# Ahead of a chunked recurrence: gate tables loaded during the projections, a growing recurrence, pipelined key products, first loads by need, key squares on ScalarE

## What is computed

```python
q, k, v = silu(hs @ Wq + bq), silu(hs @ Wk + bk), silu(hs @ Wv + bv)      # per token, 16 heads x 64
beta, fd, sd, fg, sg = five sigmoid gates per token and head
q = q * rsqrt(sum(q * q) + 1e-6);  k = k * rsqrt(sum(k * k) + 1e-6)
def step(S_f, S_s):                                                        # for each token
    S_f, S_s = fd * S_f, sd * S_s
    S_f = S_f + beta * k (v - k S_f);  S_s = S_s + beta * k (v - k S_s)
    S_fc, S_sc = cap(S_f + rf * S_s), cap(S_s + rf * S_f)
    o = fg * (q S_fc) + sg * (q S_sc)
```

## Time and profile before

| | us |
|---|---|
| runs, median of 3 | 3804.21 |
| profiled execution | 3796.57 |
| its span | 3794.8 |
| projections, first to last SiLU | 359.7 to 665.8 |
| gate stage, barrier to barrier | 688 to 970 |
| chunk loop, first PE instruction to last output | 1000 to 2777 |
| the rest of both layers behind it | 2777 to 3795 |

### The profile page before, as it was taken

The page is one execution under the profiler, slowest core; times in us unless marked ns, Lnnn a source line. Parts: engine busy times, 40 slices in busy tenths (PEclk is TensorE's granted clock), DMA queues, the critical chain, the costliest instruction groups (busy, mean ns, idle before and its releaser), DMA issues. The chain is left out here.

```text
span 3794.8 us, 75132 instructions
## 1 busy us (share of the span) xinstructions
PE 3016.8 (79%) x27767; PEld 2120.4 (56%) x27767; DVE 2638.0 (70%) x4556; ACT 1536.5 (40%) x3399; POOL 1485.2 (39%) x2134
## 2 busy tenths in 40 slices
PE   0666998572299998999989999999947368999898
PEld 0444433462277777777777777777737264333334
DVE  8895777399257775687847777566668737777775
ACT  0233888352033333333323333333325244555554
POOL 0000777473245554455545555455545513000000
PEclk9776999776589998899979998799979689999999
DMA  1001555654412321322232132122246342101111
GB/s 28 0 1 40 219 221 221 164 123 132 134 31 60 75 58 36 77 58 68 44 76 56 37 77 61 45 58 61 59 136 232 106 120 47 26 18 25 19 18 31
DMA packets 434170, 293.76 MB, mean 77 GB/s; under 512 B 335099, under 2 KB 396091, under 8 KB 425021
## 3 DMA queue, kind: packets, MB, share of 16 engines
q1 hardware_dynamic: 418976, 263.98, 24.9%
q0 software_dynamic: 10240, 8.41, 1.5%
q10 hardware_dynamic: 4608, 16.78, 1.4%
HBM read 159.59 MB, written 129.45 MB: 76 GB/s over the span
## 5 line engine op out<-in xcount | busy, mean ns | idle before, releaser
L2346 DVE TENSOR_REDUCE mx<-banks 128x2 f32<-128x1024 f32 (+3 forms) x384 | 360.4, 955 | 149.7 <-PE banks L1817 111.3
L2052 ACT ACTIVATE probs<-banks 128x1024 f32<-128x1024 f32 (+3 forms) x384 | 309.9, 810 | 287.0 <-PE banks L1839 156.6
L1083 ACT COPY xs<-banks 64x64 f32<-64x64 f32 (+2 forms) x640 | 166.2, 260 | 610.1 <-PE banks L924 607.1
L1573 POOL TENSOR_TENSOR prj_sq<-prj 128x1024 f32<-128x1024 f32 x64 | 218.2, 3428 | 389.8 <-ACT prj L1958 389.8
L924 PE MATMUL banks<-xc,ssm 64*64 64x16 f32 (+2 forms) x5120 | 262.3, 222 | 53.4 <-issue 43.1
L957 PE MATMUL banks<-stk,tw 128*128 128x192 f32 x1024 | 270.4, 423 | 38.8 <-DVE tw L1286 38.8
L802 POOL TENSOR_SCALAR xc<-xc,halves 128x64 f32<-128x64 f32 (+1 forms) x256 | 137.0, 535 | 411.0 <-DVE xc L1288 381.1
L924 PEld LDWEIGHTS banks<-xc,ssm 64*64 64x64 f32 x5120 | 220.6, 140 | 130.3 <-issue 67.7
L1288 DVE SCALAR_TENSOR_TENSOR xc<-xc,halves,banks 64x64 f32<-64x64 f32 (+1 forms) x512 | 160.4, 313 | 189.6 <-PE banks L935 185.6
L1700 PE MATMUL banks<-wproj,xnT 128*128 128x512 f32 x512 | 266.5, 602 | 20.3 <-ACT prj L1958 19.3
L1111 ACT COPY ah<-banks 128x768 f32<-128x768 f32 x128 | 102.2, 799 | 386.5 <-PE banks L957 386.5
(11 more groups left out here) (355 smaller groups left out, 7184.8 us busy)
## 6 DMA issues: line engine op xcount, KB each, us to landing
proj_s<-prj SPq DMA_DIRECT2D x32, 2048.0 KB, 6.3
qkv_t<-proj_s SPq DMA_DIRECT2D x32, 1536.0 KB, 6.7
ka<-proj_s ACTq DMA_DIRECT2D x32, 512.0 KB, 4.1
mem_s<-o_sb SPq DMA_DIRECT2D x32, 512.0 KB, 2.6
om<-mem_s SPq DMA_DIRECT2D x32, 512.0 KB, 3.9
om<-proj_s SPq DMA_DIRECT2D x32, 512.0 KB, 4.9
blk_s<-res SPq DMA_DIRECT2D x16, 512.0 KB, 4.6
rt_src<-r_s SPq DMA_DIRECT2D x512, 8.0 KB, 4.7
```

Of the source, the lines that this page charges most:

```text
L1573: pool.tensor_tensor(prj_sq[:, w, :], x, x, ALU.mult).then_inc(p_sq, 1)
L2052: act.activation(probs[:, s % 2, :, at:at + w], slot_of((kind, s, k))[:, :, 0:w], ACT.Exp, scale=D1 ** -0.5).then_inc(b_read, 1)
L2346: dve.tensor_reduce(mx[:, s % 2, c, :, t:t + 1].rearrange("p e a -> p (e a)"), slot_of((kind, s, k))[:, :, 0:w], AX, ALU.max).then_inc(a_r ...
```

## The change

- Gate loads move into the projections: after each of the first 16 tile stores SP issues four of them, `rf_c` comes with the weights, and the save of `res` comes ahead of the stores. The partition order becomes (odd or even head, pair, block). `gu` gets memory of its own.
- The key squares move from POOL to ACT, behind the fifth SiLU of a tile. `vv` is scaled in two parts (tiles 0 to 27 early), and PE's turns wait part by part.
- The gate recurrence runs over `w = 2 + t` columns in step t instead of all 18; POOL clears `gl` at the end of the projections. `lx` and its 4 MB store are gone: the two left rows are stored as they are (`l_s`), and the left factors of a tile are loaded into a cleared `lt_` by 16 small DMAs. `pc` and `yp` become seven prefix products `pq`, a masked sum and a correction. `invert(1)` leaves the stage; all parts from 1 on are inverted in the loop, in groups 0 to 10 of the 16 before their use.
- Key products: `kta` has two buffers, PE turns tile i + 1 before it multiplies tile i, ACT copies only the four 32 x 32 diagonal pieces (eight copies of 32 x 256), and POOL stores a tile with one DMA. A part is then loaded by 32 DMAs in place of one.
- The loads of tiles 0 and 1, and of `bd`, move into the gate stage, each after what it needs, and POOL's memsets move there with them. A tile's load is cut differently: 1 + 2 + 16 + 1 + 8 + 2 = 30 DMAs.
- Constants (`bmask`, `halves`, `rf_abs`, `one_rf`) are made ahead of the projections.

```diff
 # projections, SP
+            sp.dma_start(res_s, res[:, :, :].rearrange("p t d -> p (t d)")).then_inc(res_out, 16)
+            sp.wait_ge(g_stored, 16)
             for i in range(T):
                 ...
                 sp.dma_start(ps_v[i], prj[:, i % 4, :]).then_inc(p_stored[i % 4], 16)
+                for n in range(4 * i, min(4 * i + 4, 4 * H0)):
+                    k, h = n // H0, n % H0
+                    row = NB * (H0 // 2 * (h % 2) + h // 2)
+                    sp.dma_start(gu[row:row + NB, k, :, :], gates_s[(k + 1) * H0 + h, :].rearrange("(t j o) -> j t o", j=NB, o=SUB)).then_inc(gu_in, 16)
 # projections, POOL: one square instead of two, then
+            pool.wait_ge(p_silu, 8 * T)
+            pool.memset(gl[:, :, :, :], 0.0).then_inc(cc_set, 1)
 # projections, ACT
+                        if n == 4:
+                            act.wait_ge(p_silu, 8 * i + 4)
+                            act.activation(prj_sq[:, 1, :], prj[:, i % 4, HD:2 * HD], ACT.Square).then_inc(p_sq_q, 1)
 # gate stage, DVE, step t
-                seq.link(dve.tensor_tensor(ca[:, 0], src[:, 0], fd_, ALU.mult))
+                seq.link(dve.tensor_tensor(ca[:, 0, :, 0:w], src[:, 0, :, 0:w], fd_, ALU.mult))
 ...
-                seq.link(dve.tensor_tensor(gl[:, :, :, t], ca[:, 0], ca[:, 1], ALU.add))
+                seq.link(dve.tensor_tensor(gl[:, :, 0:w + 1, t], ca[:, 0, :, 0:w + 1], ca[:, 1, :, 0:w + 1], ALU.add))
 ...
-            invert(1)
 # a part's blocks, SP
-                sp.dma_start(nb, nblk_s[PT * c:PT * c + PT, :, :].rearrange("t u n -> u t n")).then_inc(nb_in, 16)
+                for j in range(NB):
+                    q, part_ = j // 2, slice(SUB * (j % 2), SUB * (j % 2) + SUB)
+                    for t in range(PT):
+                        sp.dma_start(nb[j:P:NB, t, :].rearrange("h (s o) -> h s o", o=SUB), nblk_s[PT * c + t, q, part_, :, part_].rearrange("s h o -> h s o")).then_inc(nb_in, 16)
 # gate stage, PE
+            turn_keys(0)
+            for i in range(T):
+                if i + 1 < T:
+                    turn_keys(i + 1)
+                key_products(i)
 # gate stage, ACT, copies of one tile
+                    for q in range(4):
+                        rows = slice(32 * q, 32 * q + 32)
+                        act.copy(ssa[rows, n, 8 * y:8 * y + 8, :].rearrange("p (h e) t -> p e h t", e=2),
+                                 banks[rows, 1024 + 1024 * y:2048 + 1024 * y].rearrange("p (e h t) -> p e h t", e=2, t=P)[:, :, :, rows]).then_inc(ss_kept, 1)
 # gate stage, POOL
+            for i in range(T):
+                n = i % 2
+                pool.wait_ge(ss_kept, 8 * i + 8)
+                pool.dma_start(nblk_s[i].rearrange("q r h o -> (q r) (h o)"), ssa[:, n, :, :].rearrange("p h o -> p (h o)")).then_inc(nblk_out[n], 16)
+                if i == ZERO_AT:                       # 22
+                    pool.wait_ge(gate_out, 32)
+                    pool.memset(cft[:, :, :], 0.0).then_inc(zero_set, 1)
+                if i in (ZERO_AT + 2, ZERO_AT + 4):
+                    y = (i - ZERO_AT) // 2 - 1
+                    pool.memset(blk[:, y, :, :, :], 0.0).then_inc(zero_set, 1)
 # gate stage, SP, in this order: load bd (24), load_tokens of tiles 0 and 1, load_part(0), pb and pball,
 # store gl and l_s, store_part(0), load_left x2, load_part(1), wait zero_set 3, load_blocks x2,
 # wait gate_set 1, store r_s of tiles 0 and 1, load_right x2, store the rest of r_s, wait gate_set 2,
 # 8 + 2 coefficient stores, wait for them, load_ends x2, pcb (2)
 # loop, SP, ahead of load_tile(i)
-                if i % PT == PT - 2 and 2 * PT - 2 <= i < T - PT:
-                    c = (i + 2) // PT
+                if i % PT == 0:
+                    c = i // PT
                     store_part(c)
                     if c + 1 < T // PT:
                         load_part(c + 1)
-                if i % PT == 0:
-                    sp.wait_ge(inv_out, 32 * (i // PT + 1))
+                    sp.wait_ge(inv_out, 32 * (c + 1))
                 load_tile(i)
 # loop, DVE: rows of the inverse of part k // 16 + 1 behind group k, q = k % 16
+        INVERSE = ((1, 2, 3), (4, 5, 6), (7, 8), (9,), (10,), (11,), (12,), (13,), (14,), (15,))
```

More of the change, by code:

```diff
@@ L668, in chunk_sync @@
+            sp.wait_ge(lm_set, MASKS)
+            for i in range(2):
+                load_left(i)
+            sp.wait_ge(inv_out, 32)
             load_part(1)
+            sp.wait_ge(zero_set, 3)
+            for i in range(2):
+                load_blocks(i)
             sp.wait_ge(gate_set, 1)
-            sp.dma_start(r_s.rearrange("h j r t s -> (h j) (r t s)"), rb[:, :, :, :].rearrange("p r t s -> p (r t s)")).then_inc(gate_out, 16)
-            sp.dma_start(l_s.rearrange("h (i r) t n -> (h i) (r t n)", r=2), lx[:, :, :, :, :].rearrange("p r t j o -> p (r t j o)")).then_inc(gate_out, 16)
@@ L672, in chunk_sync @@
[L672 to L679, removed]
@@ L680, in chunk_sync @@
-            end_phase(sp)
+            for first_, end in ((0, 2), (2, T)):
+                sp.dma_start(r_s[:, :, :, first_:end, :].rearrange("h j r t s -> (h j) r (t s)"), rb[:, :, first_:end, :].rearrange("p r t s -> p r (t s)")).then_inc(gate_out, 16)
+                if first_ == 0:
+                    sp.wait_ge(gate_out, 48)
+                    for i in range(2):
+                        load_right(i)
+            sp.wait_ge(gate_set, 2)
+            for e in range(2):
+                for k, src in enumerate((gam[:, 0], gam[:, 1], cend[:, 0], cend[:, 1])):
+                    sp.dma_start(cf_s[e, k].rearrange("g j t o -> (g j) (t o)"), src[64 * e:64 * e + 64].rearrange("p t o -> p (t o)")).then_inc(gate_out, 16)
@@ L1053, in chunk_act @@
+            for i in range(2):
+                load_keys(i)
+            keep_turned_keys(0)
+            for i in range(T):
+                if i + 1 < T:
+                    keep_turned_keys(i + 1)
+                keep_key_blocks(i)
             end_phase(act)
@@ L1189, in chunk_dve @@
             for m in range(2):
[L1190 to L1191 removed]
+                seq.link(dve.tensor_copy(pb[:, :, 2 * m:2 * m + 2], last[:, m, :, 0:2]))
+            dve.tensor_copy(glc[:, :, :, :], gl[:, :, 0:2, :]).then_inc(pb_set, 1)
             dve.wait_ge(pb_set, 1)
@@ L1245, in chunk_dve @@
             dve.wait_ge(lm_set, MASKS)
-            for lv in range(LEVELS):
-                q = P // (2 * SUB << lv)
-                seq.link(dve.tensor_reduce(half4[:, :, 0:q], ident[:, :].rearrange("p (q a t) -> p a q t", q=q, a=2), AX, ALU.add))
-                seq.link(dve.tensor_reduce(halves[:, lv, :], half4[:, :, 0:q], AX, ALU.add))
-            dve.scalar_tensor_tensor(out=rf_abs[:, :], in0=rf_c[:, :], scalar=-1.0, in1=rf_c[:, :], op0=ALU.mult, op1=ALU.max).then_inc(rf_set, 1)
+            dve.wait_ge(zero_set, 4)
@@ L1318, in new_state @@
                     dve.wait_ge(z_mm, k + 1)
+                if k == 4 and step == 0:
+                    dve.wait_ge(pc_in, 32)
                 if first(k):
```

364 lines of the change are left out of this document (183 added, 181 removed).

## The result

| | us | ratio to before [95% interval] |
|---|---|---|
| before, median beside it | 3803.88 | |
| after, median of 4 runs (3705.07 to 3714.81) | 3712.27 | 0.9754 [0.9737, 0.9771] |
| predicted | 3653, 3605 to 3700 | |

What follows compares the result with a forecast made beforehand. Bounds: a circle through GpSimd's key square in the projections, DVE's chain in the gate stage, PE in the loop. 174 us gained before the loop less 23 lost in it, 151 off 3796.6, plus 7.6 for the median: 3653, range 3605 to 3700.

Steps and rivals of the forecast that it cites:

- Key squares on ACT: Projections: ACT becomes the bound at 8.95 us a tile, 19.5 us saved, plus 2.5 in the last tile; no table loads.
- Tail: End of the projections: 7 us instead of 11.9 from DVE's last product to the barrier, 4.9 saved.
- Gate chain: Gate stage on DVE: recurrence 68.4 us against 101.5 before, chain ending 151 us after the stage starts.
- Key products and SP: Gate stage: key products 4.9 us a tile, ending at S + 165; SP's queue bounds the stage at S + 179.
- rival A: Gate stage: key products keep their old pace, 6.1 us a tile, zero_set 3 comes 32 us later: 3685; chance 0.2.
- Late by 0 to 10 each, I take 3: +18: Loop, tiles 4, 8, ..., 24: part loads delay the tile's reload 3 us each, 18 us lost, from 0 to 60.
- slack of 7.5: Loop reloads: 7.5 us between the landing of a tile's loads and PE's turn, the other five 6 to 11.
- The inverse of part 1 in the loop: Loop: 21.7 us of new DVE work, mostly hidden, costing 5 us, from 0 to 12.
- B: Loop: the reload queue is 13 us late instead of 3 at six tiles, +60: 3713; chance 0.13.
- C: Loop, first-tile groups: PE's clock stays up, nine groups gain 4.5 us each, 40 in all: 3613; chance 0.14.
- D: Projections don't shorten, ACT still waiting for GpSimd through the value squares, +22: 3675; chance 0.06.
- E: Loop: the tile's load lasts 36 us instead of 22, 6.5 late at 30 tiles, slower than before: 3830; chance 0.03.

Runs made afterwards that it cites:

- e3: The changed kernel with the key squares back on GpSimd: 3730.72 us, ratio 0.9811.
- e8: e5 and e6 together, with GpSimd's clearing of lt, ssm and sqr spread over tiles 1 to 4 of the key products: 3574.10 us, ratio 0.9296.
- e5: e1 with part 1 loaded behind the gate stage's last barrier, inverse rows one group later, clearing of cft and blk earlier: 3641.26 us, ratio 0.9488.
- e1: The changed kernel with a tile's own loads issued ahead of the next part's 32 loads: 3617.40 us, on another chip 3650.43, ratio 0.9502 both times.
- e7: The changed kernel with 24 of a part's 32 loads ahead of the tile's loads and 8 behind: 3676.22 us, ratio 0.9674.
- e6: e1 with first-tile groups also issuing the 12 products of other groups, into columns nothing reads: 3584.25 us, ratio 0.9332.

## Why the prediction was wrong

- *Key squares on ACT: right.* 8.95 us a tile forecast, 8.85 measured, no idle in front of the root; e3 gives 25 us at the stage's start for 22 forecast. The Square brought no table load.
- *Tail: right in sum.* Barrier at 659.4, forecast 661.6. It opens 8.8 us behind DVE's last product (650.59), where I took 7; the tiles, 0.1 us shorter each than forecast, made up for it.
- *Gate chain: 153.6 us from the barrier, forecast 151.* The recurrence took 71.5 for 68.4, and nearly the whole difference, 3.0, is one copy that stood behind GpSimd's memsets (e8).
- *Key products and SP: the sum right, the parts not.* A tile took 4.46 us (GpSimd's stores run from 674.55 to 812.82, 31 tiles), forecast 4.9, so rival A did not come, and the blocks were cleared at 796.9, 10 us earlier than the forecast 806.6. SP could not use it: it issued the loads of part 1 until 803.40, which would have been hidden at the later time that I had forecast, and took 41.4 us for the rest where I had 34. PE at 845.25, forecast 841. In e5, without the part loads there, PE starts 6 to 7 us earlier.
- *"Late by 0 to 10 each, I take 3: +18": the step that failed.* The six groups cost 96.6 us. Three things went into it.
  - The choice of 3. With the slack of 7.5 that I read in the earlier trace rows and 3.5 saved on the tile's load, my own terms give 17 to 21 - 3.5 - 7.5 = 6 to 10 a tile, 8 in the middle; the 3 had no row behind it. That is 30 us for six tiles.
  - The price of an issue. It was 23.88/32 = 0.746 us, above both bounds that I had set (0.54 and 0.66), so 23.9 us and not 17 to 21. By the same terms that makes 12.9 a tile, and the measured wait is 12.1: some 25 us more for six tiles.
  - The price of a stall, which I counted as its length. Each also lost the clock, 4 us, 24 in all. The prediction put nothing for it.

  What covers the part loads was right in sum: 3.5 + 7.5 = 11.0 us by the prediction, 23.9 - 12.8 = 11.1 measured at tile 4. Its parts were other. The tile's load takes 18.1 us (1062.82 to 1080.90) where it took 23.0 before (1196.59 to 1219.58), 4.9 less and not 3 to 4. In e1, with nothing ahead of it, that load begins only at 1040.75, 3.6 us behind the issue of the inverse's store, whose landing SP waits for; in the kernel after the part loads cover this wait. And the slack left in e1 is 6.8 us: its last issue ends at 1059.57 and lands some 1.7 us later (as 1080.90 and 1082.56 in the kernel after), and PE turns at 1068.06. e1 and e7 show waits and clock together: 0, 24 and 32 loads ahead of the tile give 0, 58.8 and 96.6 us.
- *The inverse of part 1 in the loop: +5 forecast.* Not seen: e1 has it, and its loop from PE's start to the last `ah` copy takes 1752.9 us against 1755.5 before. Something else made the loop shorter by a few us, and a cost of the inverse as small may be hidden under it; no run takes the two apart.
- *Rivals.* B was the mechanism, and had the wait right (13 us, 12.1 measured). Its loop came to 23 + 60 = 83 against 90: it left out the 24 us of clock, counted 5.5 too much for the waits (78 against 72.5) and 5 for the inverse, and nothing for the 7 us that the rest of the loop gained. That its 3713 is the measured time is in part luck: between the profiled executions it would give 3705.6 against 3714.8, and the 7.6 us added for the median hide that. It had a chance of 0.13, and only half of it was let into the range. C did not happen: the first-tile groups kept 0.60 though no dense row of the inverse stands before them any more; e6 shows that the clock there rises with PE's own work, though not in every group. D is refuted by the tile of 8.85, E by the tile load of 18.1 us.

## What to carry to other kernels

In a queue that issues in order, the price of an added transfer is paid by what stands behind it: before you add one, put in order what each entry is needed for, and when; here two lines exchanged were worth 95 us, more than the whole change had gained. When an issue price is bounded from rows of other transfers, let the range reach beyond the late end (here 0.75 us came out where the rows gave 0.54 to 0.66), and take the middle of your own terms and not the happy end. Add to each stall of TensorE what the lost clock costs, here 4 us for stalls of 3.4 to 13.1 us alike. A stretch of light TensorE work at a low clock can be slower than the same stretch with products added that nobody needs.

## What the runs showed of the hardware

- Issue of small loads from the SP queue: a load of 256 pieces of 64 bytes cost 0.746 us in the loop of the kernel after (0.70 in the gate stage and in e1's loop), 0.64 in a run of eight (5.12 us, e7); at the same reload a left-factor load cost 0.54 (8.66/16) and a block load 0.62 (4.99/8). The 22.4 to 23.9 us for the 32 loads of a part lie a little above the 21 that the prediction estimated with each piece counted as 512 bytes. No run varied the size of the pieces, so whether pieces or issues set the price stays open.
- A float32 copy of 64 columns on DVE stood still until the last of GpSimd's memsets had ended (661.11 to 664.31 against 664.24), and took 0.22 us without them. Products with two inputs, 659.95 to 661.1, ran beside GpSimd at their normal 0.23 us. In the other direction, GpSimd's memset of 9216 columns took 7.78 us beside a DVE product of 3.36 us, not longer than by its size, while its square, which reads, had taken 5.09 beside that product instead of 1.89 without it, and 2.43 with 0.7 us of it. The Trainium skill (SBUF — State Buffer, Who interferes with whom) has a pair of ports that either engine locks for a whole instruction, for DVE by copies among others, and by a product with two inputs only against a GpSimd instruction that reads. These rows agree; that the copy got no turn between one memset and the next is shown here alone.
- PE's clock: 127 records in 17 us at 0.60, 151 in 11.8 at 1.00 (e6, but with exceptions at 0.64 to 0.67 there and in e8). After stalls of 3.4 to 7.9 us (e7) and of 10.6 to 13.1 (the kernel after) PE lost the same 4 us on top, working at 0.50 before it was granted 1.00 again. The Trainium skill (TensorE: Matmul & The Clock Gate, HAM oscillation) describes such a loss for PE that waits for DMA in every round of a loop; the six stalls here agree. That adding products wins the clock back over a run of groups is shown here by e6 alone.
